# Two GpSimd memsets of an unused tile behind every second group of gathers

## What is computed

```python
def _gcn_conv(x, src, dst, ew, W, b, n_nodes):
    xW = x @ W
    deg = segment_sum(ew, dst) + 1.0
    dinv = rsqrt(deg)
    norm = dinv[src] * ew * dinv[dst]
    agg = segment_sum(norm[:, None] * xW[src], dst)
    return agg + (dinv * dinv)[:, None] * xW + b
# x = x + relu(conv2(relu(conv1(layernorm(x)))))
# x = x + moe(layernorm(x)): 8 experts, the best 2 of each token, 256 -> 256 (gelu) -> 256, plus the tokens
```

## Time and profile before

| | |
|---|---|
| median of three runs | 5221.11 us (5214.46 to 5225.19) |
| profiled execution, own time | 5177.12 us |
| its span, first to last instruction | 5175.3 us |
| busy over the span | PE 74%, PE weight load 68%, POOL 58%, DVE 44%, ACT 14% |
| granted TensorE clock, mean | 0.855 |
| chain that ended last, by engine | PE 28%, DVE 19%, POOL 18%, issue 16%, another core or an unknown queue 14% |

### The profile page before, as it was taken

One profiled execution on the slowest core, in us unless ns is written; L12 is line 12 of the kernel. 1 busy time (PEld: TensorE's weight loads), 2 busy tenths in 40 slices (PEclk: granted clock), 3 DMA queues, 4 the chain that ended last, 5 costly groups with the idle time before them and its releaser, 6 DMA issues.

```text
span 5175.3 us, 82233 instructions
## 1 busy us (share of the span) xinstructions
PE 3841.7 (74%) x27222; PEld 3496.5 (68%) x27223; DVE 2298.3 (44%) x8827; ACT 722.4 (14%) x2277; POOL 3003.7 (58%) x3241
## 2 busy tenths in 40 slices
PE   3445565555555555555558999999999999999999
PEld 3424454554555545555557899889989899988998
DVE  6732222222222222222224655566556655656655
ACT  1020000000000000000001222222222222222222
POOL 0104666666666666666666666666666666656663
PEclk9998766766666666667668999999999999999999
DMA  3244333333333333333333333333333333333332
GB/s 95 62 144 122 99 97 97 100 96 98 98 97 100 96 97 99 95 98 98 97 94 93 95 97 99 96 96 96 96 98 96 96 97 98 96 93 95 95 97 59
DMA packets 243540, 500.39 MB, mean 97 GB/s; under 512 B 61453, under 2 KB 141656, under 8 KB 243179
## 3 DMA queue, kind: packets, MB, share of 16 engines
q0 software_dynamic: 150528, 411.24, 28.0%
q1 hardware_dynamic: 87210, 79.56, 4.9%
q10 hardware_dynamic: 5440, 5.01, 0.3%
HBM read 456.90 MB, written 38.67 MB: 96 GB/s over the span
## 4 chain that ended last, share of the span: by engine, by line
PE 28%; DVE 19%; POOL 18%; issue 16%; another core or an unknown queue 14%; DMA 3%; DVEq 2%; SPq 1%; ACT 0%; POOLq 0%; ACTq 0%
POOL msg L461 18%; PE part L736 11%; DVE sel L1047 5%; PE psY L730 5%; PE psH L721 3%; PE psY L736 3%; DVE mix L1175 2%; PE psH L736 2%; DMA msg<-ytab,srcT 1%; DVEq L272 1%; DVE accbuf L1055 1%; DVE accbuf L989 1%; DVE nt L1129 1%; PE psT L689 1%
## 5 line engine op out<-in xcount | busy, mean ns | idle before, releaser
L461 POOL DMA_INDIRECT msg<-ytab,srcT x3136 | 2968.1, 946 | 1878.2 <-issue 962.3
L736 PE MATMUL part<-sel,msg 128*128 128x96 f32 x8384 | 1155.9, 293 | 255.6 <-issue 207.9
L736 PEld LDWEIGHTS part<-sel,msg 128*128 128x128 f32 x8384 | 1113.6, 210 | 310.6 <-issue 270.1
L730 PE MATMUL psY<-w_s,hS 128*128 128x256 f32 x3136 | 838.1, 390 | 19.6 <-DVE mix L1175 10.1
L1047 DVE TENSOR_SCALAR sel<-iota,relT,ewT 128x96 f32<-128x96 f32 x3136 | 838.6, 342 | 2.5 <-ACT accbuf L514 1.6
L721 PEld LDWEIGHTS psH<-tokS,w_s 128*128 128x128 f32 x6272 | 811.3, 192 | 36.1 <-issue 0.5
L721 PE MATMUL psH<-tokS,w_s 128*128 128x128 f32 x6272 | 813.9, 275 | 0.4 <-issue 0.4
L1055 DVE TENSOR_TENSOR accbuf<-accbuf,part 128x192 f32 x524 | 185.6, 354 | 1215.8 <-remote 744.3
L553 ACT ACTIVATE hS<-psH,b_s 128x128 f32<-128x128 f32 x1568 | 487.7, 362 | 1411.9 <-PE psH L721 798.6
L730 PEld LDWEIGHTS psY<-w_s,hS 128*128 128x128 f32 x3136 | 543.3, 191 | 113.7 <-issue 64.3
L736 PE MATMUL psH<-sel,msg 128*128 128x96 f32 x2080 | 370.0, 335 | 251.4 <-issue 232.6
(11 more groups left out here) (167 smaller groups left out, 2024.8 us busy)
## 6 DMA issues: line engine op xcount, KB each, us to landing
msg<-ytab,srcT POOLq DMA_INDIRECT x3136
msg<-in_x SPq DMA_DIRECT2D x194, 128.0 KB, 2.1
ytab<-xS SPq DMA_DIRECT2D x99, 128.0 KB, 15.2
ytab<-msg SPq DMA_DIRECT2D x98, 128.0 KB, 1.7
xS<-in_x SPq DMA_DIRECT2D x98, 128.0 KB
out<-res SPq DMA_DIRECT2D x98, 128.0 KB
w_s<-in_L_ffn_w ACTq DMA_DIRECT2D x2, 2048.0 KB
accbuf<-in_dst SPq DMA_DIRECT2D x1, 588.0 KB
```

The source lines that it names most:

```text
L461: pool.indirect_dma_start(msg[:, r * GT + j, :], None, ytab[l], bass.IndirectOffsetOnAxis(ap=srcT[:, g * GT + j:g * GT + j + 1].bitcast(U3 ...
L730: mm = pe.matmul(psY[e % 2][:, 0:D], hS[:, e % 2, m, :], w2_s[:, e, m, :], start=(m == 0), stop=(m == KD - 1))
L736: m = pe.matmul(slot[:, h * W:(h + 1) * W], msg[:, tile0 + j, h * P:(h + 1) * P], sel[:, sel0 + j, :], start=(j == 0), stop=(j == GT - 1))
```

## The change

Behind the four gathers of every second group of the first layer (n = 1, 3, ..., 391), POOL fills the two halves of `hS` with zeros. Each fill waits for the one before it, and ACT waits for all of them before it starts on the second layer.

```diff
@@ semaphores
+    s_rest = sem("s_rest")
@@ block.gpsimd, in the loop over n, behind the four indirect_dma_start of group n
+                if l == 0 and n % 2 == 1:
+
+                    for u in range(2):
+                        wait(pool, s_rest, n // 2 * 2 + u)
+                        pool.memset(hS[:, u, :, :], 0.0).then_inc(s_rest, 1)
@@ block.scalar, between the first and the second layer
+        act.wait_ge(s_rest, NG // 2 * 2)
```

## The result

The changed kernel takes 5228.69 us (median of 20 runs, 5224.67 to 5244.71), the kernel before in the same comparison 5220.6 us (20 runs, 5214.09 to 5227.81). The ratio is 1.002 with an interval of 1.0013 to 1.0027: slower by 8 us, or 0.2%. The forecast was 5221 us and no difference; the time lies in the stated range of 5105 to 5335, the direction was missed.

What follows compares the result with a forecast made beforehand. The first layer was taken as bound by a rate limit of 1.436 us a gather, with 2.97 us of POOL waiting a turn. Fills of 2.2 us a turn add 0 to 5175.3; carrying over the median's 44 us gives 5221, range 5105 to 5335.

Steps and rivals of the forecast that it cites:

- POOL arrives later at a wait that ends when it ended before: First layer: fills of 2.2 us a turn (1.6 to 2.7) stay under POOL's wait and cost nothing.
- the cover: POOL's real waiting in each first-layer turn, 2.97 us; fills beyond it would cost 98 us for each us more.
- rival B: The end of POOL's wait follows its last gather, so fills are added: 216 us, 5437 (157 to 265); chance 0.07.
- rival A: Pauses behind fills free PE's held-back signals; turns of 22.2 us, 75 us faster, 5146 us; chance 0.27.
- a rate limit of 1.436 us a gather: First layer: 22.97 us a turn over 16 gathers, whatever stands behind it; POOL's added time is absorbed by its wait.
- what a fill takes from the thing that limits the rate: Unpriced load of fills on the first layer's limit: between nothing and 1.24 us a turn, 122 us; taken as nothing.
- rival C: A fill loads what limits the rate: up to 1.24 us a turn, 5343 us; a fifth of it 5246; chance 0.12.
- 0.3 us of late gather: Late, longer second gather at two trace places; 0.3 us more POOL time left the pace unchanged, so fills were priced at nothing.
- the pair: Two fills behind every second group: 0.87 us plus 0.25 for a slower next gather, taken as 1.1 (0.8 to 1.35).
- 0.25 us for a cold first gather: Gather behind a pair of fills may be slower, as the first of all was (1.14 and 1.00 against 0.95): +0.25 us.
- Rival D: Fills and DVE exclude each other: each fill waits for a 0.34 us selection, 59 us over the cover, 5280; chance 0.06.
- Rival E: Each change between gather and fill reloads code; a microsecond instead of 0.25 us gives 3.7 us a turn, 5293; chance 0.02.

Runs made afterwards that it cites:

- the two later ones: Changed kernel (two fills) against the kernel before: 5183.29 us, ratio 1.0007, on chip 8; 5177.98 us, ratio 1.0009, on chip 5 in a later round.
- chip 7: First-round place without POOL's long wait: kernel before 4755.18 us, two fills 4864.71 (1.0231), four fills 5009.61 (1.0533), half products 4756.09 (1.0001).
- chips 7 and 11: Places without POOL's long wait; on chip 11 kernel before 4754.96 and 4756.61 us, two fills 4864.26 (1.0226), an eighth of the products 4746.41 (0.9982).
- chips 8 and 5: Places with POOL's long wait: kernel before 5179.99 us on chip 8, 5219.34 and later 5173.61 on chip 5; ten fills on chip 8 5586.44 (1.0786).

## Why the prediction was right or wrong

**Right: the fills are hidden by POOL's wait.** The step "POOL arrives later at a wait that ends when it ended before" held with two and four fills, and ten fills showed the rest of their time beyond the cover, to 1 us in 407. This also excludes rival B, the wait that follows the last gather. Against rival A stands that no run with fills was faster.

**Right: a rate limit of 1.436 us a gather.** It was read from runs of 12, 16 and 20 gathers. Leaving out half of PE's work gave 28 us in all, at most 0.3 us a turn of the 2.9 that it would give if PE set the pace. What the limit is, this doesn't tell. It holds only where the long wait is, and loosely: 1.428 us a gather with half of PE's work, 1.450 in the first profile of the changed kernel.

**Wrong: "what a fill takes from the thing that limits the rate ... I take nothing".** This is the term that failed, and in size it is a fifteenth of rival C's upper price: 8 us in the first comparison, 3 and 4 in the two later ones, and 10.6 for four fills, where 122 was kept as the end for two. The working rested on 0.3 us of late gather, once at each of two places of the trace. The pace read there scatters from 1.433 to 1.436 us a gather, which is 0.05 us a turn; 8 us are 0.08 us a turn. As the first comparison's interval excludes no change, the forecast of none was wrong, by 8 us. Whether it is rival C's mechanism stays open, and so does what in a fill costs this. The prediction's sign for C, turns of 23.2 us or more, stands in the first profile (23.20) and in neither of the two later ones (22.98). Fills of one column cost 2.7 us and full ones 3.3 in the same round, so nothing says that it is the writing; and neither differs from zero there.

**Mis-sized: the pair.** 1.1 us was forecast, with ends 0.8 and 1.35; it takes 0.55. A fill has 0.32 us as worked out (0.30), but the start behind a gather costs nothing, the wait between two fills 0.06 and not 0.17, and the gather behind it does not start late but early, 0.15 us after the fill in place of 0.30. The 0.25 us for a cold first gather was not there. On a chip without cover this error would have doubled the answer. Under the cover it had no effect.

**Not seen: that the cover belongs to the place.** The prediction took the wait for a property of the kernel. It said that the cover is thin, and named no case in which it is missing. The price there is 109 us, 2.3%. So it was luck that the first comparison fell on a place with the wait. The profile gave two signs: 99 waits whose releaser the profile could not name, and signals that came 6 us behind the instruction that sends them. The same program on another chip has neither.

**Rival D, the shared port.** It said that each fill waits for a selection. The selections of DVE take 342 ns each in the earlier trace rows, as they do over both layers before the change, and 344 ns over both layers in the changed kernel:

```profile
L1054 DVE TENSOR_SCALAR sel<-iota,relT,ewT 128x96 f32<-128x96 f32 x3136 | 840.4, 344 | 2.5 <-ACT accbuf L520 1.6
```

In its first layer 56 pairs of fills stand beside selections and take 0.70 us on average, as do the 128 pairs beside which DVE does nothing. Here is one:

```profile
596.96 0.69 POOL L468 MEMSET hS<- 128x256 f32 x2
597.00 1.05 DVE L1054 TENSOR_SCALAR sel<-iota,relT,ewT 128x96 f32<-128x96 f32 x4
```

So fills do not wait for selections. Some interference there is, mostly at DVE's cost, and clearest in another instruction. On chip 7 DVE's scaling of the table (L1118, 128 x 256) takes 0.35 us at least and up to 0.86 where a gather and a fill stand beside it:

```profile
1272.34 0.95 POOL L462 DMA_INDIRECT msg<-ytab,srcT  x1 [0.30 <-issue]
1272.54 0.86 DVE L1118 TENSOR_SCALAR xS<-lin,dinv 128x256 f32<-128x256 f32 x1
1273.29 0.72 POOL L468 MEMSET hS<- 128x256 f32 x2
```

In the kernel before on that chip the same instruction takes up to 0.60 us beside gathers alone. The 33 pairs of fills that stand beside L1118 and nothing else of DVE's take 0.76 us on average there, in place of 0.70. This is far from the 0.34 us a fill that the rival needs. (The Trainium skill, SBUF — State Buffer, "Who interferes with whom", has a GpSimd instruction that only writes blocked by VectorE instructions in a two-port mode alone; whether these are in one no run here shows.)

**Rival E, a reload of code at every change from gather to fill.** It would show in front of the gather behind the fill, which starts after 0.15 us. The length of the first gather, which the prediction named against it, could not show a load that comes before the gather, as 157.64 us of idle time stand there.

## What to carry to other kernels

Added work on an engine costs only what exceeds its wait, so first ask how steady that wait is: if its releaser is unnamed, or answers long after the instruction that sends the signal, get a second profile from another chip before counting on it. Test a cover by overfilling it: ten fills told more than any finer look at two. Compare profiles only where their spans differ by what the timed runs differ by.

## What was not expected of the hardware

One program has two paces. On chips 7 and 11 a gather of 128 rows of 1 KB is issued every 1.253 us, with the kernel before at 4755 to 4756 us; on chips 8 and 5 every 1.436 to 1.437 us with two fills, with the kernel before at 5174 to 5219 us. The issue of one gather takes the same time at both, about 0.95 us and a gap of 0.30. What the slower pace adds is PE's late signals and 0.7 us steps between its instructions. The second layer takes 2346 to 2350 us in the profiles of one kind and 2480 to 2525 in those of the other. The DMA engines are not what is slow: their busy share is 0.34 of a turn of 22.98 us and 0.39 of 20.05, 7.8 us in both. Nor is it PE's clock, at least in the second layer. There the granted clock is 1.00, its upper level, at both paces, and PE still does fewer instructions in the same 500 us, first at the slower pace (rows of the kernel before), then at the faster one (the same kernel on chip 7):

```profile
3500.00:4000.00 500.00, 485.70 (x3501) 451.69 (x3500) 299.10 (x1171) 121.83 (x405) 305.59 (x324) 1.00 0.34 97
```

```profile
3500.00:4000.00 500.00, 500.00 (x3665) 471.31 (x3664) 317.80 (x1229) 127.65 (x423) 323.68 (x338) 1.00 0.35 101
```

What holds PE's signals back was not found.
